# A two-image patch-attention kernel: half-width embedding from x by row parity, column copies on ScalarE, later keys, two patch chunks sent from GpSimd's queue

## The reference

```python
x = x + L0(gn(x))                # gn: each channel of each image by its own mean and deviation
x = x + dct2(gn(x))              # 48-point cosine transform over height and width

def L0(x):                       # x: [2, 32, 48, 48]
    embed_w  = prelu(conv1x1(x, Wa, ba), aa)         # 32 channels
    match_in = prelu(conv1x1(x, W1, b1), a1)         # 16 channels
    raw_w = extract_patches(embed_w, 6, 2)           # 576 patches
    ref = prelu(conv1x1(x.reshape(B, C, 24, 2, 24, 2).mean((3, 5)), W2, b2), a2)
    w = extract_patches(ref, 3, 1)                   # 576 keys of 16 x 3 x 3
    wn = (w / maximum(norm(w), 1e-4)).reshape(B, 576, 144)
    xp = extract_patches(match_in, 3, 1).reshape(B, 2304, 144)
    yi = softmax(10 * einsum('blc,bqc->blq', wn, xp), axis=1).reshape(B, 576, 48, 48)
    yt = transposed_conv(yi, raw_w)                  # stride 2, 6x6
    return (conv3x3(yt, Wd, stride=2) + bd) / 6
```

## Time and profile before

| | us |
|---|---|
| median of 3 runs (218.26 to 219.45) | 218.42 |
| the profiled execution | 218.58 |
| its span, first to last instruction | 216.8 |
| TensorE busy | 183.7 |
| VectorE busy | 143.0 |
| GpSimd busy | 123.7 |
| ScalarE busy | 114.6 |

### The profile page before, as it was taken

The page is one execution under the profiler, slowest core; times in us unless marked ns, Lnnn a source line. Parts: engine busy times, 40 slices in busy tenths (PEclk is TensorE's granted clock), DMA queues, the critical chain, the costliest instruction groups (busy, mean ns, idle before and its releaser), DMA issues.

```text
span 216.8 us, 3530 instructions
## 1 busy us (share of the span) xinstructions
PE 183.7 (85%) x1142; PEld 148.8 (69%) x1142; DVE 143.0 (66%) x292; ACT 114.6 (53%) x212; POOL 123.7 (57%) x110
## 2 busy tenths in 40 slices
PE   0396739999998785899999999899759998899993
PEld 0343529897896672788888888788538775677890
DVE  6659896649647799655656757676983299578112
ACT  4866644568768790876463747374531364142300
POOL 7445220269997894599895999999779300001000
PEclk9999555999999999999999999999985999998555
DMA  6192057665440000354775420000046000004312
GB/s 164 28 222 57 2 96 127 101 174 114 74 76 0 0 5 0 49 93 82 189 215 94 76 50 0 3 0 0 2 102 172 0 0 0 5 0 84 60 22 54
DMA packets 15239, 14.06 MB, mean 65 GB/s; under 512 B 9302, under 2 KB 12950, under 8 KB 15030
## 3 DMA queue, kind: packets, MB, share of 16 engines
q1 hardware_dynamic: 13878, 13.03, 29.0%
q10 hardware_dynamic: 1344, 0.82, 1.3%
HBM read 2.14 MB, written 1.18 MB: 15 GB/s over the span
## 4 chain that ended last, share of the span: by engine, by line
PE 64%; DVE 22%; issue 6%; ACT 4%; ACTq 2%; DVEq 0%; POOL 0%; POOLq 0%
PE yt L969 14%; PE zt L953 11%; PE ps L927 8%; PE pm L927 4%; DVE mimg L1392 4%; PE ps L953 3%; PE zt L989 3%; DVE v L1523 2%; PE zt L927 2%; ACTq L379 2%; PE pm L876 2%; PE yt L876 2%; PE pm L865 2%; DVE negm L1456 2%; PE yt L865 2%
## 5 line engine op out<-in xcount | busy, mean ns | idle before, releaser
L732 POOL TENSOR_TENSOR nt<-nt 128x599 f32<-128x599 f32 (+1 forms) x51 | 69.1, 1355 | 9.1 <-ACT nt L1170 5.7
L969 PE MATMUL yt<-yf,kf 125*128 125x384 f32 (+1 forms) x120 | 50.3, 503 | 7.4 <-DVE yf L1475 6.4
L953 PEld LDWEIGHTS zt<-ident,nt 128*125 128x125 f32 (+1 forms) x300 | 39.5, 178 | 12.0 <-issue 2.6
L953 PE MATMUL zt<-ident,nt 128*125 128x128 f32 (+1 forms) x300 | 41.5, 275 | 0.0
L1170 ACT ACTIVATE nt<-nt,rps 128x599 f32<-128x599 f32 x31 | 24.6, 794 | 7.0 <-DVE rps L1463 7.0
L1475 DVE COPY yf<-zt 125x384 f32<-125x384 f32 (+1 forms) x28 | 19.3, 691 | 10.9 <-PE zt L953 10.7
L969 PEld LDWEIGHTS yt<-yf,kf 125*128 125x128 f32 (+1 forms) x120 | 19.0, 195 | 9.0 <-DVE yf L1475 7.2
L1182 ACT ACTIVATE yf<-zt 125x384 f32<-125x384 f32 (+1 forms) x22 | 15.2, 690 | 18.0 <-PE zt L953 18.0
L1161 ACT ACTIVATE nt<-ps,negm 128x576 f32<-128x576 f32 x20 | 14.6, 732 | 14.6 <-DVE negm L1456 14.6
L927 PE MATMUL ps<-wh,vh 128*128 128x288 f32 x40 | 12.2, 388 | 6.4 <-ACT nt L1161 3.7
L689 POOL TENSOR_TENSOR mv<-mv,mhalf 32x1 f32<-32x1 f32 x2 | 1.1, 542 | 27.7 <-DVE mv L1265 27.7
(11 more groups left out here) (196 smaller groups left out, 378.5 us busy)
## 6 DMA issues: line engine op xcount, KB each, us to landing
nt<-nt SPq DMA_DIRECT2D x12, 285.2 KB, 4.4
vh<-mimg SPq DMA_DIRECT2D x24, 72.0 KB, 2.5
vl<-mimg SPq DMA_DIRECT2D x24, 72.0 KB, 2.5
v<-x SPq DMA_DIRECT2D x2, 288.0 KB, 4.0
v<-vr SPq DMA_DIRECT2D x2, 288.0 KB, 5.3
vh<-mimg SPq DMA_DIRECT2D x12, 48.0 KB, 2.2
vl<-mimg SPq DMA_DIRECT2D x12, 48.0 KB, 2.3
x_copy<-v SPq DMA_DIRECT2D x2, 288.0 KB, 2.7
```

What stands on the lines that cost most here:

```text
L732: pool.tensor_tensor(nt[:, dst, (to + 1) * KP + 1:(to + 1) * KP + 1 + n], nt[:, one, (row1 + 1) * KP + 1:(row1 + 1) * KP + 1 + n], nt[:, o ...
L953: last = nc.tensor.matmul(turned(sums_bank(m), n, column), keys_at(tile, r + dr, n, shift), ident[:, :], start=at == 0, stop=at == len(wor ...
L969: nc.tensor.matmul(yt[:, k % 2, 0:CHUNK], kf[b][0:n, blk, :], yf[0:n, blk, :], start=blk == 0, stop=blk == KB - 1).then_inc(s_mb, 1)
```

## The change

- The embedding reads x from a second copy in SBUF, split by the parity of the pixel row and by half image (in the space of kf, which is written later). Eight loads on SP bring it (four per image). The rows of both parities stand on 64 partitions, so a half image needs two matmuls of 288 columns. The weight tile wae has 160 columns instead of 896; a small tile umask is summed beside the other masks.
- For image 1 "columns_before" runs on ScalarE, in front of "after".
- "match" of image 1 starts at gap 20 with pace 1.6 (VectorE's parts from step 7), "keys" of image 1 at gap 39 with pace 3 (36 and 2 before).
- GpSimd's queue issues the 12 DMAs of the high and low patches of image 0's chunks 4 and 5 (far_patches), with semaphores of their own; SP keeps the others.
- Of the first group's turned sums ScalarE copies block 4 as well; "wait_copied" counts by the table.

```diff
-WIDE = 7 * C
+WIDE = 5 * C
...
+FAR = 4
...
-    ("bias_a", 1, 1, 16, 1), ("norm", 1, 1, 17, 1), ("emb", 1, 2, 21, 3), ("match", 1, 8, 24, 1.5), ("ek", 1, 2, 28, 1),
-    ("inorm", 1, 2, 31, 1), ("dup", 1, 1, 35, 1), ("after", 1, 1, 36, 1), ("keys", 1, 2, 36, 2),
+    ("bias_a", 1, 1, 16, 1), ("norm", 1, 1, 17, 1), ("emb", 1, 2, 21, 3), ("match", 1, 8, 20, 1.6), ("ek", 1, 2, 28, 1),
+    ("inorm", 1, 2, 31, 1), ("dup", 1, 1, 35, 1), ("after", 1, 1, 36, 1), ("keys", 1, 2, 39, 3),
...
+        def eight_taps(eng, t, high_in, low_in):
+
+            pitch = mimg.shape[1]
+            for low, dst, done in ((0, vh, high_in), (CR, vl, low_in)):
+                for k, (dx, n) in enumerate(SHIFTS):
+                    src = F(mimg[32 * k + low:32 * k + low + CR, :])
+                    src = bass.AP(src.tensor, src.offset + match_rows_at(1 + dx, t, 0), [[pitch, CR], [BLOCK, n], [1, CHUNK]])
+                    eng.dma_start(F(dst[3 * CR * k:3 * CR * k + n * CR, CHUNK * t:CHUNK * (t + 1)]), src).then_inc(done, 16)
+
         def arrived(eng, landed, g, images):
 
-            eng.wait_ge(landed[g], 16 * (len(NINTH) if landed is s_vr else len(SHIFTS)) * images)
+            if landed is not s_vr and g >= FAR:
+                eng.wait_ge((s_farh if landed is s_vh else s_farl)[g - FAR], 16 * len(SHIFTS))
+                images -= 1
+            if images:
+                eng.wait_ge(landed[g], 16 * (len(NINTH) if landed is s_vr else len(SHIFTS)) * images)
...
+        def parity(b):
+
+            return kf[b][:, :, :].rearrange("p k c -> p (k c)")[:, 0:QUARTER]
...
-            return blk % 2 or k >= NG - LAG and blk == KB - 1
+            return blk % 2 == 1 or (k == 0 or k >= NG - LAG) and blk == KB - 1
...
+            def load_parity(b):
+
+                for h in range(2):
+                    for u in range(2):
+                        src = strided_rows(x[b], HL * h + u)
+                        dst = parity(b)[2 * C * h + C * u:2 * C * h + C * (u + 1), :].rearrange("c (h w) -> c h w", w=W)
+                        sp.dma_start(dst, src).then_inc(s_xu[b], 16)
...
-                for low, dst, done in ((0, vh, s_vh[t]), (CR, vl, s_vl[t])):
...
+                if b or t < FAR:
+                    eight_taps(nc.sync, t, s_vh[t], s_vl[t])
...
+            for b in range(B):
+                load_parity(b)
             sp.dma_start(cosm[:, :], dct).then_inc(s_cos, 16)
...
+            def far_patches():
+
+                pool.wait_ge(s_before[0], 2)
+                pool.wait_ge(s_after[0], 2)
+                for t in range(FAR, NCH):
+                    eight_taps(nc.gpsimd, t, s_farh[t - FAR], s_farl[t - FAR])
...
             output_weights()
             pool.wait_ge(s_wd, 1)
+            far_patches()
...
-                v = x4[b][:, :].rearrange("p (i u j v) -> p i u j v", u=2, j=WL, v=2)
-                for r in range(2):
-                    for n in range(4):
-                        at = C * (3 - n)
-                        last = nc.tensor.matmul(o[:, REFQ * r:REFQ * (r + 1)], wa4[:, 2 * i + r, at:at + 128],
-                                                v[:, :, n // 2, :, n % 2], start=n == 0, stop=n == 3)
+                rows = slice(2 * C * i, 2 * C * (i + 1))
+                for v in range(2):
+                    at = C * (1 - v)
+                    last = nc.tensor.matmul(o[:, 0:HALF], wae[rows, at:at + 4 * C], strided(parity(b)[rows, :], v, (2, HALF)),
+                                            start=v == 0, stop=v == 1)
...
+                if b:
+                    columns_before(nc.scalar.copy, b, first, n)
...
-                link(nc.vector.memset(wa4[:, :, :], 0.0))
+                link(nc.vector.memset(wae[:, :], 0.0))
...
+                link(nc.vector.tensor_tensor(umask[:, :], smask[:, 1, 0:2], smask[:, 1, 2:4], ALU.add))
...
-                dve.wait_ge(s_dup[b], 2)
-                columns_before(b, NEAR, BLOCKS - NEAR)
+                if not b:
+                    dve.wait_ge(s_dup[b], 2)
+                    columns_before(nc.vector.tensor_copy, b, NEAR, BLOCKS - NEAR)
```

41 lines of the change are left out of this document (21 added, 20 removed).

## The result

The changed kernel is slower: 220.05 us, the median of 20 executions, against 217.62 of the kernel before beside it. The ratio is 1.0118, with a 95% interval of 1.0081 to 1.0155, so some 2.6 us; forecast were 4.2 us less. A time here is the median of all executions of a run, while a ratio and its interval leave out, on both sides, the executions more than 1.5% above the fastest of their kernel, so the two need not agree. An execution's time goes with TensorE's mean granted clock: the changed kernel took 218.2 us at 0.906, 220.5 at 0.883, 225.4 at 0.878.

A forecast was written before the change was run, and what follows sets the result against it. TensorE bounds 40 to 65 us, VectorE's match rows and copies the chain to 91. Exp 14 −5.3 (earlier savings included) and +1.1 behind it give −4.2; 218.58 − 4.2 − 0.16 = 214.2, said 214.3 us; own range 212.5 to 216.3, full 211.3 to 218.6.

The forecast's parts named there:

- GpSimd's DMAs: Twelve issues behind the output weights, taken at 1.0 us each, GpSimd free at 42.2; hidden up to 1.09 us an issue.
- norm 1: TensorE's step needing GpSimd's squares: reached at 52.5 us, squares ready at 51.4, so no wait.
- the rival: The other side: dear GpSimd issues make TensorE wait for squares; at 1.6 us each, net +1.9, 220.3 us; chance 0.12.
- Steps 7 to 14: Image 1's match rows: exp 8 at 57.2, exp 12 at 71.0, exp 13 at 76.1, exp 14 at 81.5, −5.3 us.
- Embedding: TensorE's two matmuls of 288 columns: 1.02 us less each, two before step 7, −2.04 us (−1.0 at the dear end).
- Prologue: Start of the kernel: smaller cleared weight tile 0.6 less, added mask sum 0.23 more; −0.37 us (−0.6 to +0.2).
- Behind exp 14: ScalarE's added copies put exp 15 4.4 us behind exp 14 instead of 3.3; past scores 17 the program is unchanged.
- the parity loads: Eight loads on SP ahead of the reference patches, 3.6 us to issue, covered by 5.5 us: no cost.
- exp 14's new releaser: On ScalarE, the copy of block 4 releases exp 14, not VectorE.
- the three signs of being wrong: TensorE waits for the squares, exp 13 comes after 77.5 us, or the stretch behind scores 17 grows.
- Scores 17: TensorE's scores of tile 17, waiting for exp 15: near 86.8 us instead of 90.97, −4.2 us.

The follow-up runs named there:

- sender_alone: The kernel before with only GpSimd's queue issuing the twelve DMAs of image 0's patches of chunks 4 and 5; 219.70 us, ratio 1.0155 to the kernel before.
- old_spread: The changed kernel with the old pace of image 1's match rows and keys; 218.21 us, ratio 1.0055 to the kernel before.
- embedding_alone: The kernel before with only the new embedding (row-parity loads, smaller weight tile, mask); 217.07 us, ratio 1.0024 to the kernel before.
- filled_gap: The changed kernel with nine unused unit-matrix products on TensorE ahead of the first tap product; 218.06 us, ratio 1.0040 to the kernel before.
- own_bank: The changed kernel with the first tap product waiting only for the two banks tap products write, not all four; 217.21 us, ratio 1.0022 to the kernel before.

## Why the prediction was wrong

**The step that failed first** is "GpSimd's DMAs". It put the sender at nothing as long as an issue takes less than 1.09 us. It priced the issues as time of GpSimd alone and asked whether norm 1 would wait. Norm 1 didn't (53.75, no idle), and the issues were cheaper than taken, 0.5 us and not 1.0. What they cost was elsewhere: SP and ScalarE issue in the same microseconds, and ScalarE's six issues stand in order ahead of exp 0. They took 5.3 to 6.2 us with that sender and 4.3 to 4.8 without; TensorE's clock mostly rose later behind them. That is 1.5 us at exp 0 and 2.4 at exp 3 (1.3 and 1.8 without the four traces named there), by seven traces against eleven; sender_alone, one of the seven, shows it with no other part of the change. The row of ScalarE's issues was in the trace of before and got no term, since they belong to no edit. The estimate from the Trainium skill's page "DMA: Bandwidth & Descriptors" (section "Latency and other measured facts"), twelve ended at 42.2, was 5 us too late: they ended at 37.4. No row shows the stretching of GpSimd's issues that the Trainium skill's page "SBUF — State Buffer" (section "SBUF: two separate sides") led me to weigh. That is no test of the rule, though: beside these issues VectorE ran no copy or cast in any of the seven traces. The sign of the rival was right, its mechanism wrong; that its 220.3 us are close to the measured 220.05 is luck.

**Steps 7 to 14.** From exp 8 to exp 13 the forecast had 18.9 us, and 18.90 was measured, in both of its parts (13.7 to exp 12 where it had 13.8, then 5.2 where it had 5.1). From exp 13 to 14 it had 5.4, measured were 7.9: the copy of block 4 was named, but the wait of TensorE's first tap product in front of it was not followed to VectorE, where the early rows put the last match row and the row copy ahead of the scaled keys. A TensorE that comes earlier opens the same gap: it is 2.07 us in old_spread, with the old rows, and 3.04 in embedding_alone, where the embedding is the only edit. Of the 2.5 us, filled_gap shows 1.6 as the half clock behind the idle stretch; own_bank shows 5.13 once the wait is gone. The change moved the wait; it didn't remove it.

**Embedding.** 1.02 us less each was forecast, 0.65 measured, the dear end of the range being 0.5; the embedding itself took 1.21 us, not 1.02, and the scores behind it lost 0.2. Ahead of step 8 the early rows' high part takes back 0.7 of the 1.3, where 0.4 was allowed. So exp 8 gained 0.7 in the first trace, not 2.0.

**Prologue.** −0.37 forecast, −0.07 measured: the smaller tile ends in a wait for the parameters, which land at 6.7 us (ScalarE's six issues start at 29.64 instead of 29.71). The prediction asked for x and not for these.

**Behind exp 14.** Exp 15 came 4.8 us behind exp 14 (4.4 forecast), but "past this the program is unchanged" overlooked the late keys: exp 14 to 18 takes 13.4 us instead of 11.8, 0.7 of it the keys and some 0.65 the column copies (12.70 with them on ScalarE, 12.05 without). From exp 18 on it is unchanged, as said.

**Right** were the parity loads at no cost, norm 1, exp 14's new releaser, and the size of exp 8 to 13. Of the three signs of being wrong none came in the first trace (norm 1 without a wait, exp 13 at 77.39, nothing longer behind scores 17): none of them watched ScalarE's issues or the first tap product. Scores 17, at 90.93 where the forecast named 86.8, spoke against it.

The sum by traces: +2.4 at exp 3; exp 3 to 13 34.2 and 34.5 us against 34.3, the embedding paid back by the order of rows; exp 13 to 18 21.3 against 21.0. Together +2.7, or +2.1 with the smaller figure for exp 3, and +2.6 measured; so the size of the first term is known to about half a microsecond. The changed kernel's own two traces are level with before and 3.8 us behind it at exp 18.

Open: why queues slow each other's issues (the share of busy DMA engines from 30 to 40 us was 0.86 against 0.67, and SP's patches issued in the same time landed after 3.9 to 5.8 us, against 2.1 to 2.7 before), and how much of the clock's late rise is chance. In kernels without that sender it rose between 35 and 39 us; with it, it was still or again at 0.5 past 41 us in five of seven traces.

## What to carry to other kernels

Price a new DMA issuer by what the other queues issue in the same microseconds, and look for compute that stands behind those issues in order; that row may belong to no edit. For each engine that an edit makes earlier, follow its next wait to the instruction that ends it, and count a long idle stretch of TensorE twice where TensorE is what the rest waits for: for itself and for the half clock that came behind it here. One trace of a kernel whose times spread by 3% proves little about 1%: compare segment by segment over several traces.
